# A cross-attention and feed-forward kernel on one core: all engines' instructions and the Sync queue's transfers in a new order

## The reference

```python
q = layernorm(x) @ Wq            # 16 heads of 32
k = ctx @ Wk; v = ctx @ Wv       # 128 keys a batch
q = ln_head(q)*gq + bq; k = ln_head(k)*gk + bk
attn = softmax(q @ k.T / sqrt(32))
x = x + (attn @ v) @ Wo
s = layernorm(x) @ Win + bin_    # 64 units
h = relu(s[..., None]*W1 + b1)   # 16 inner each
g = einsum(h, W2) + b2
x = x + g @ Wout + bout
```

## Time and profile before

| what | value |
|---|---|
| median of 3 runs | 463.92 us (461.03 to 465.71) |
| profiled execution | 462.87 us |
| its span, first to last instruction | 461.1 us |
| TensorE matmul busy | 428.3 us (93%), 2344 matmuls |
| TensorE weight load busy | 290.2 us (63%) |
| VectorE, ScalarE, GpSimd busy | 328.0, 316.5, 241.2 us |
| mean granted TensorE clock | 0.980 |
| transfers | 57.85 MB on the one queue, 47.4% of the DMA engines' time |

### The profile page before, as it was taken

One profiled execution on the slowest core, in us unless ns is written; L12 is line 12 of the kernel. 1 busy time (PEld: TensorE's weight loads), 2 busy tenths in 40 slices (PEclk: granted clock), 3 DMA queues, 4 the chain that ended last, 5 costly groups with the idle time before them and its releaser, 6 DMA issues. The chain is left out here.

```text
span 461.1 us, 7791 instructions
## 1 busy us (share of the span) xinstructions
PE 428.3 (93%) x2344; PEld 290.2 (63%) x2344; DVE 328.0 (71%) x652; ACT 316.5 (69%) x611; POOL 241.2 (52%) x326
## 2 busy tenths in 40 slices
PE   4998994996999999999999999999998999997994
PEld 2576883455658667577577756676574366546772
DVE  2887882655368699579857996659777976669674
ACT  3848954497664992899848963899658937952750
POOL 4427876177446637549545571737524724406463
PEclk9999998698899999999999999999999999999999
DMA  8454492794364204961595009703850656043004
GB/s 296 139 194 134 105 202 67 183 203 153 82 154 98 73 1 158 220 150 47 150 248 123 11 35 270 176 3 69 229 143 21 136 185 139 2 147 128 1 2 183
DMA packets 28105, 58.34 MB, mean 127 GB/s; under 512 B 8864, under 2 KB 9376, under 8 KB 24992
## 3 DMA queue, kind: packets, MB, share of 16 engines
q1 hardware_dynamic: 28064, 57.85, 47.4%
HBM read 22.18 MB, written 8.39 MB: 66 GB/s over the span
## 5 line engine op out<-in xcount | busy, mean ns | idle before, releaser
L1074 DVE TENSOR_REDUCE mx<-bank 128x4 fp32r<-128x512 f32 x128 | 82.8, 684 | 37.1 <-PE bank L2676 36.9
L1854 ACT ACTIVATE prob<-bank 128x512 f32<-128x512 f32 x128 | 71.2, 608 | 41.0 <-PE bank L2690 30.4
L2702 PE MATMUL bank<-prob,v_kv 128*32 128x512 f32 x256 | 63.3, 608 | 0.1
L2705 PE MATMUL bank<-prob,den_sel 128*32 128x512 f32 x256 | 62.6, 608 | 0.0
L1935 ACT ACTIVATE hid<-s_in,b_col,w_col 128x256 f32<-128x256 f32 x105 | 56.1, 611 | 2.2 <-DVE s_in L1135 1.9
L2613 PE MATMUL bank<-wq_hi,zt_hi 128*128 128x512 f32 x128 | 52.7, 411 | 4.6 <-DVE zt_lo L1061 4.6
L737 POOL TENSOR_TENSOR qt_lo<-u,qt_hi 128x512 fp32r<-128x512 f32 x32 | 40.4, 1286 | 27.8 <-ACT qt_hi L1839 17.5
L2613 PE MATMUL bank<-wq_hi,zt_lo 128*128 128x512 f32 x128 | 51.6, 403 | 0.0
L2613 PE MATMUL bank<-wq_lo,zt_hi 128*128 128x512 f32 x128 | 51.5, 403 | 0.0
L2690 PE MATMUL bank<-q_stack,k_stack 97*128 97x512 f32 x128 | 43.0, 425 | 8.3 <-DMA q_stack<-mxt 6.9
L742 POOL TENSOR_TENSOR at_lo<-att,at_hi 128x512 fp32r<-128x512 f32 x28 | 35.6, 1290 | 28.7 <-ACT at_hi L1904 28.7
(11 more groups left out here) (175 smaller groups left out, 903.1 us busy)
## 6 DMA issues: line engine op xcount, KB each, us to landing
q_stack<-qt_hi SPq DMA_DIRECT2D x64, 256.0 KB, 4.9
xin<-in_x_dram SPq DMA_DIRECT2D x36, 256.0 KB, 3.7
q_stack<-qt_lo SPq DMA_DIRECT2D x32, 256.0 KB, 4.8
x<-in_x_dram SPq DMA_DIRECT2D x28, 256.0 KB, 3.6
out_dram<-x SPq DMA_DIRECT2D x28, 256.0 KB, 2.2
att<-in_L_xattn_Wk_dram SPq DMA_DIRECT2D x1, 1024.0 KB, 6.4
x<-in_L_xattn_Wq_dram SPq DMA_DIRECT2D x4, 256.0 KB, 7.2
hid<-in_L_xattn_Wv_dram SPq DMA_DIRECT2D x1, 1024.0 KB, 9.7
```

The costliest lines, as they stand in the source:

```text
L1074: dve.tensor_reduce(mx[:, :].rearrange("p (g i j) -> p g i j", g=G, i=HC)[:, :, 2 * half + r, j], maxs_banks[T][half][j][r][:, :].rearrang ...
L1854: act.activation(prob[:, h % PR, :], score_bank[t][h][:, :], ACT.Exp, scale=SCALE).then_inc(exp_done, 1)
L2702: pe.matmul(at_bank[t][c][rows(n), :], v_kv[kv_of(t)][:, n * HD:(n + 1) * HD], prob[:, n % PR, :], start=True, stop=True)
L2705: ins = pe.matmul(den_bank[t][rows(n + 2), :], den_sel[:, c, :], prob[:, n % PR, :], start=c == 0, stop=c == C - 1)
```

## The change

The steps, their instructions and their waits for data stay what they are; each engine calls the same steps in another order, the PSUM tables give other banks, and TensorE's waits for free banks go with them. Each list holds the same steps as before, on TensorE 577, on VectorE 562, on ScalarE 584, on GpSimd 197, on SP 138 (after the fixed beginning).

The Sync queue in its first stretch, and one row of each kind of the other changes:

```diff
             def part1():
                 load_params()
-                load_wo()
                 load_x(1, 0)
...
                 load_x(1, 3)
+                load_wo()
...
                 stack_q(0, 3)
-                stack_keys(1)
-                stack_max(0)
                 load_x(3, 0)
                 load_x(3, 1)
                 load_x(3, 2)
                 load_x(3, 3)
+                stack_max(0)
                 stack_q(1, 0)
                 stack_q(1, 1)
                 stack_q(1, 2)
                 stack_q(1, 3)
-                load_wout()
-                stack_max(1)
                 load_x(4, 0)
                 load_x(4, 1)
-                load_x(4, 2)
-                load_x(4, 3)
+                stack_max(1)
                 load_residual(0, 0)
+                stack_keys(1)
                 load_residual(0, 1)
                 load_residual(0, 2)
+                load_residual(0, 3)
+                load_wout()
+                load_x(4, 2)
                 stack_q(2, 0)
+                load_x(4, 3)
                 stack_q(2, 1)
-                load_x(5, 0)
-                load_residual(0, 3)
                 stack_q(2, 2)
...
         z1_bank = banks_of([
-            (2, 3, 2, 4),
+            (2, 3, 1, 2),
...
                 z1_low(3, 1)
+                z1_low(3, 2)
                 rden_error(0)
                 rden_fix(0)
                 rden_split(0)
-                stats1(4, 0)
-                z1_low(3, 2)
-                stats1(4, 1)
```

More of the change, by code:

```diff
@@ L236, in build_program @@
[L236 to L239, removed]
+        den_bank = [banks[n] for n in (7, 7, 2, 1, 5, 4, 3, 2)]
+        s_bank = [banks[n] for n in (5, 4, 3, 3, 2, 7, 4, 1)]
+        rstd_bank = [banks[n] for n in (0, 5, 0, 4, 0, 6, 3, 0)]
+        sum_bank = {T: banks[n] for T, n in ((6, 4), (7, 1),)}
+        win_mean_bank = banks[4]
@@ new lines, in part4 @@
+                spread(0, 0)
+                pe.wait_ge(qf_done, 11)
+                pe.wait_ge(qt_hi_done, 11)
+                max_scores(2, 1, 1)
+                pe.wait_ge(u_done, 15)
+                scores(1, 1)
+                pe.wait_ge(mx_done[1], 18)
+                scores(1, 2)
+                pe.wait_ge(exp_done, 17)
+                scores(1, 3)
+                spread(0, 1)
+                spread(0, 2)
+                pe.wait_ge(exp_done, 18)
+                spread(0, 3)
@@ L2988, in part4 @@
+                pe.wait_ge(mx_done[1], 19)
+                scores(1, 4)
+                pe.wait_ge(exp_done, 19)
+                turn_q(2, 3)
+                pe.wait_ge(att_done, 1)
+                turn_z1(3, 3)
+                pe.wait_ge(mx_done[1], 20)
+                pe.wait_ge(exp_done, 20)
+                values(1, 0)
+                values(1, 1)
                 pe.wait_ge(qf_done, 12)
                 pe.wait_ge(qt_hi_done, 12)
-                scores(1, 0)
-                pe.wait_ge(u_done, 13)
@@ L3038, in part5 @@
                 scores(1, 11)
+                project_o(0, 0, 0)
+                project_o(0, 0, 1)
+                pe.wait_ge(mx_done[0], 20)
+                scores(1, 12)
+                pe.wait_ge(exp_done, 27)
+                project_o(0, 1, 0)
+                project_o(0, 1, 1)
+                pe.wait_ge(exp_done, 28)
+                scores(1, 13)
+                pe.wait_ge(u_done, 16)
+                project_o(0, 2, 0)
+                project_o(0, 2, 1)
+                pe.wait_ge(att_moved, 6)
@@ L3189, in part7 @@
+                pe.wait_ge(exp_done, 44)
+                scores(2, 15)
                 pe.wait_ge(exp_done, 45)
-                scores(2, 14)
-                scores(2, 15)
-                pe.wait_ge(att_moved, 11)
-                max_scores(3, 1, 1)
+                max_scores(3, 1, 2)
                 pe.wait_ge(exp_done, 46)
-                max_scores(3, 1, 2)
+                pe.wait_ge(mx_done[1], 27)
+                max_scores(3, 1, 3)
+                pe.wait_ge(mx_done[1], 28)
+                turn_q(4, 0)
@@ L3409, in part11 @@
                 pe.wait_ge(exp_done, 72)
+                scores(4, 8)
                 values(4, 2)
                 values(4, 3)
+                pe.wait_ge(g_done, 3)
+                pe.wait_ge(mx_done[1], 41)
+                project_y(2, 0)
+                pe.wait_ge(exp_done, 73)
+                project_y(2, 1)
+                pe.wait_ge(mx_done[1], 42)
+                pe.wait_ge(att_moved, 18)
+                max_scores(5, 1, 1)
+                pe.wait_ge(out_done, 9)
+                project_o(3, 1, 0)
@@ L3422, in part11 @@
+                pe.wait_ge(mx_done[1], 44)
                 project_o(3, 2, 0)
                 project_o(3, 2, 1)
+                pe.wait_ge(mx_done[0], 48)
+                project_o(3, 3, 0)
+                pe.wait_ge(mx_done[1], 46)
                 pe.wait_ge(x1_done, 13)
+                max_scores(5, 1, 3)
+                scores(4, 9)
                 scores(4, 10)
[L3426 to L3428 removed]
@@ L3458, in part11 @@
                 pe.wait_ge(z2t_done, 15)
-                turn_q(6, 0)
-                pe.wait_ge(exp_done, 80)
                 turn_q(6, 1)
+                values(4, 6)
+                values(4, 7)
+                pe.wait_ge(zt_lo_done, 29)
+                project_s(3)
+                pe.wait_ge(att_moved, 20)
+                spread_rstd(3)
+                pe.wait_ge(zt_lo_done, 30)
+                turn_z1(7, 2)
+                turn_z1(7, 3)
                 pe.wait_ge(z2t_done, 16)
@@ L3607, in part14 @@
+                max_scores(7, 1, 0)
+                pe.wait_ge(z2t_done, 20)
                 spread(5, 0)
-                pe.wait_ge(z2t_done, 19)
-                max_scores(7, 0, 0)
-                pe.wait_ge(z2t_done, 20)
+                pe.wait_ge(mx_done[0], 57)
+                spread(5, 1)
+                pe.wait_ge(exp_done, 97)
                 project_s(4)
+                pe.wait_ge(exp_done, 98)
+                spread_rstd(4)
+                pe.wait_ge(mx_done[1], 58)
+                scores(6, 2)
@@ L3612, in part14 @@
+                scores(6, 3)
+                pe.wait_ge(att_done, 22)
+                max_scores(7, 0, 1)
+                pe.wait_ge(rstd_moved, 5)
+                spread(5, 2)
                 pe.wait_ge(qf_done, 32)
                 pe.wait_ge(qt_hi_done, 32)
-                spread_rstd(4)
+                pe.wait_ge(exp_done, 99)
+                max_scores(7, 1, 1)
+                pe.wait_ge(exp_done, 100)
                 pe.wait_ge(mx_done[0], 58)
-                spread(5, 1)
-                pe.wait_ge(exp_done, 98)
@@ L3630, in part14 @@
                 scores(6, 5)
-                values(6, 1)
+                scores(6, 6)
                 pe.wait_ge(mx_done[1], 59)
                 pe.wait_ge(exp_done, 101)
-                max_scores(7, 0, 1)
+                max_scores(7, 1, 2)
+                pe.wait_ge(mx_done[1], 60)
+                spread(5, 3)
                 pe.wait_ge(exp_done, 102)
-                scores(6, 6)
-                pe.wait_ge(mx_done[1], 60)
-                values(6, 2)
-                pe.wait_ge(exp_done, 103)
```

2076 lines of the change are left out of this document (1006 added, 1070 removed), and 32 rows, old and new, of tables (maxs_rows, score_bank).

## The result

The changed kernel takes **444.1 us** (median of 4 runs, 442.05 to 448.21) against 463.7 us (461.03 to 465.71) for the kernel before beside it: ratio 0.959, 95% interval 0.950 to 0.968. Run twice more on other occasions it gave 444.1 and 444.5 us (0.961 both times).

What follows compares the result with a forecast made beforehand. TensorE was taken as the bound from 118.2 to 280 us, with time winnable only where it idles or runs at half clock. Terms -8.7 - 6.5 + 2.5 + 1.5 - 0.9 = -12.1 gave 451.8 us, range 446 to 460.

Steps and rivals of the forecast that it cites:

- First gap: TensorE idle 6.78 us before scores(0,0), then half clock: 9.7 us removed, 1.0 back for a late row max, -8.7 us.
- Second gap: TensorE idle 3.89 us at 109 us, then half clock; z1_low(3,2) ahead of block 4's statistics removes it, -6.5 us.
- new waits: Between 75 and 125 us other engines must keep up with an earlier TensorE: +2.5 us, bounds 0 and 6.5.
- (a): Possible wait at turn_q(2,0), now 16.7 us of work behind block 2's last projection: 0 to 2 us.
- (b): Possible wait at scores(1,0), 13.7 us of work behind scores(0,15), with q's stack, loads and row max between: 0 to 2 us.
- (c): Second batch of keys queued behind load_residual(0,0), block 1's exponentials waiting behind att_high(0,0): 0 to 2 us.
- Row max of block 2: Before scores(2,0), 9.6 us of work must cover an 11.3 us path; 1.7 us missing, taken as +1.5.
- Slower: Rival, chance 0.06: late row max in blocks 0, 2, 4, 6, 7 costs 7.2 us each; 469 us from three on.
- Start: Selectors first on VectorE, x of block 1 ahead of Wo on the queue: 0, between -1 and +1 us.
- Behind 280 us: Waits of 0.9 and 1.0 us go, one new 1.0 comes, 4.0 us of waits for x remain: -0.9 us.
- From the profiled execution to the median: The median of the runs was taken to lie 1.05 us above the profiled execution, 450.8 to 451.8 us.
- Better: Rival, chance 0.07: no new wait at all, 445.8 us.

Runs made afterwards that it cites:

- one, where the gap alone was 7.9: Kernel before with the second batch of keys behind the first residual load and stats1(4,0) to (4,3) behind normalise(0,3): 457.0 us, ratio 0.992.
- the experiment above: Changed kernel with diagonal(8) to (10) back ahead of residual1(6,0) and load_residual(4,3) back behind the row max of block 6: 450.3 us, ratio 0.975.

## Why the prediction was right in direction and wrong in size

By its own terms, against the windows of the two profiles (idle time, and work at half clock):

- **First gap, -8.7:** right. Idle time fell by 6.4 us, and the 2.95 us of half clock went with it: -9.4. The 1.0 us put back for a late row max did not come, nor did it in the two repeated profiles.
- **Second gap, -6.5, and new waits, +2.5:** right together, -3.9 for -4.0. The new waits are 2.6 us. Of the three named, (a) and (b) cost nothing, and (c), keys, `att_high` and the exponentials behind it, is what happened. That the -6.5 could be had by the one step named was wrong, though: the experiments show that the wait goes to the next in line.
- **Row max of block 2, +1.5:** it cost 0. I had the path from the last matmul to the turn at 4.0 us; it took 2.1 (143.2 to 145.3), since VectorE came to its reductions at once, and the eight pieces took 4.97 instead of 5.90. That was the lower end of this term. What I had priced at block 2 came, in the repeated profiles, at block 6: 1.6 and 2.2 us, for which the sum had no term, though the rival "Slower" named that block.
- **Start, 0:** -0.6, within its bounds (in the repeated profiles -1.1 and -1.3, just outside). Between 180 and 280 us a wait of 0.5 is new (2.0 and 0.7 us of idle time in the repeats).
- **Behind 280 us, -0.9: the step that failed.** It was -4.6 in the profiles (-3.7 and -3.3 with the repeated ones, idle for 11.3 and 11.7 us there). The sentence was "The 4.0 us of waits for `x` remain, the steps ahead of them being the same." They were not the same. The step waited for (`residual1`) kept its neighbours on TensorE, but on VectorE three steps that had stood ahead of it were behind it, and on the Sync queue its load had passed a row max. I had compared the orders at the two large gaps alone. Undone in the changed kernel, the two moves cost some 6 us (5.9 between the medians).
- **From the profiled execution to the median, +1.05:** it was -1.4. The sum was 450.8 for the profiled execution, which took 445.5, and 451.8 for the median, which is 444.1. So of the 7.7 us by which I was off, 5.3 are in the trace and 2.4 in where one profiled execution lies among its runs. That offset is no property of a kernel: the kernel before had medians of 461.1 to 463.7 us on the five occasions here.

Of the 5.3 us in the trace, 3.7 are the late waits, 1.5 the row max of block 2, 0.7 the first gap and 0.6 the start, less 0.5 for the new wait behind 180 us, 0.5 for work at half clock (TensorE's busy time fell by 5.1 us, not 5.55) and 0.1 for the new waits. "Better", with a chance of 0.07, was nearest in size at 445.8, but it too kept the waits for `x`.

The bound of 6.5 us for a new gap was about right for most of the other orders, where new gaps of 3.3 to 4.4 us cost at least 2.2 us more by the clock, and too low for one, where the gap alone was 7.9. The changed order has no such gap.

## What to carry to other kernels

When a change reorders whole lists, look at every wait of the trace, and for each at what stands ahead of the awaited step **on its own engine and queue** in both orders; that a step's neighbours on the waiting engine are the same says nothing. A gap priced at its full length is worth that only if the next waiter has slack: where several engines wait for the same queue, moving one step moved the gap here, and of the orders tried only the new order of all of them removed it. Put transfers that an engine waits for next ahead of those that nobody needs yet, and look at what the transfer at the head of the queue itself waits for, since all behind it wait too.

## What the runs showed that I had not expected

**Small VectorE steps beside GpSimd's.** A `diagonal` step (128x128, from memory to memory) takes 0.25 to 0.28 us alone. Beside GpSimd's `att_low` (1.25 us each, memory to memory) the three took 1.01, 1.31 and 1.29 us, each ending about with one of GpSimd's, and as tensor-tensor 1.09, 1.36 and 1.34, while `residual1` and `normalise`, which read one operand from a bank, kept their 0.68 beside the same work. The Trainium skill (SBUF — State Buffer, "SBUF: two separate sides") says that GpSimd shares a port pair with a VectorE instruction that has two SBUF inputs or runs in a mode that takes both ports, that whichever starts first holds it for its whole length, and that the other is fully blocked; the trace agrees.

**The clock behind short gaps.** I had taken from before that gaps up to 2.5 us leave the clock at 1.00. Over all profiles here, behind 60 us, by the mean over the 4.5 us that begin half a microsecond behind a gap: every gap of 3.34 us or more was followed by work at 0.50 (means of 0.50 to 0.73); of two gaps of 3.27 and 3.31 us neither was; and of fifteen gaps between 2.0 and 2.8 us six left the clock at 1.00 and nine were followed by a mean of 0.62 to 0.74, the same wait at `turn_z2(6,0)` among both kinds. One profile that shows 1.00 behind such a gap is no proof for the next run: a wait of 2.5 us is worth 2.5 to some 4 us. The window behind it in the kernel before (2.54 us), to be held against that of the experiment above (2.56 us, 0.62):

```profile
420.10:424.60 4.50, 4.50 (x28) 3.80 (x27) 4.50 (x8) 0.63 (x1) 2.35 (x2) 1.00 0.00 2
```
